# Products of weights with weights, written to idle PSUM banks, in TensorE's waits

## The reference

```
x = x + xattn(ctx_1024, layernorm(x), mask, ...)        # 2048 + 128 keys, 16 heads of 64
x = x + attn(layernorm(x), qw, kw, vw, ow)              # 16 heads of 32, causal, rotary
x = x + ffn(layernorm(x), ...)                          # see below
# ffn: mlp = silu(h @ Wg + bg) * (h @ Wu + bu) @ Wd + bd          (inner width 2048)
#      q = h @ Wq ; sim = q . keys ; top 8 of 64 on two sides, top 8 of their 64 sums
#      experts = sum over the 4 x 8 chosen of silu(h . down[i]) * softmax(score) * up[i]
#      returns mlp + experts
```

## Time and profile before

| | |
|---|---|
| median of 3 runs | 902.45 us (900.21 to 902.87) |
| the profiled execution: its own time | 903.4 us |
| the profiled execution: span | 901.6 us |
| mean granted TensorE clock over the span | 0.977 |
| TensorE busy | 855.2 us, 95% of the span, 6297 matmuls |
| VectorE, ScalarE, GpSimd busy | 64%, 49%, 39% |

### The profile page before, as it was taken

How to read it: one execution, slowest core, us unless ns; L and a number is a source line. 1 busy time by engine, 2 the same in 40 slices (tenths; PEclk the granted TensorE clock), 3 DMA queues, 4 the chain that set the end, 5 groups by cost and what they waited for, 6 DMA issues and landing times.

```text
span 901.6 us, 17320 instructions
## 1 busy us (share of the span) xinstructions
PE 855.2 (95%) x6297; PEld 800.6 (89%) x6297; DVE 581.5 (64%) x1540; ACT 437.5 (49%) x1017; POOL 349.0 (39%) x362
## 2 busy tenths in 40 slices
PE   3999999999999999999999999999998789998997
PEld 2899999999999999999999999999878689996885
DVE  7455557566577877665565666777766347755885
ACT  4575554554556564545446464445416024334652
POOL 5723634534464656446454523333002010003442
PEclk9999999999999999999999999999996779999999
DMA  5446336465466677675655656877577255932310
GB/s 189 167 155 199 134 107 233 177 241 218 177 233 239 218 256 259 215 254 189 245 183 211 233 189 229 329 272 259 192 282 336 77 214 218 375 135 95 113 48 24
DMA packets 71110, 183.04 MB, mean 203 GB/s; under 512 B 6337, under 2 KB 19569, under 8 KB 65009
## 3 DMA queue, kind: packets, MB, share of 16 engines
q1 hardware_dynamic: 70928, 181.90, 56.5%
q10 hardware_dynamic: 96, 0.02, 0.0%
HBM read 130.00 MB, written 50.86 MB: 201 GB/s over the span
## 4 chain that ended last, share of the span: by engine, by line
PE 81%; DVE 8%; issue 4%; ACT 3%; DMA 2%; POOL 1%; SPq 0%; DVEq 0%; ACTq 0%; POOLq 0%
PE pJ L1621 14%; PE pJ L1623 14%; PE pJ L1622 14%; PE pV L1751 7%; PE pS L1729 4%; PE pT L1737 3%; PE pS L1737 3%; PE pT L1729 2%; PE pS L1621 2%; PE pS L1623 2%; PE pS L1622 2%; PE pX L1652 1%; DVE late L1578 1%; PE pV L1621 1%; DMA WS<-w_split 1%
## 5 line engine op out<-in xcount | busy, mean ns | idle before, releaser
L1621 PE MATMUL pJ<-WV,XT 128*128 128x256 f32 x544 | 158.6, 292 | 0.1
L1622 PE MATMUL pJ<-WV,XT 128*128 128x256 f32 x544 | 153.8, 283 | 0.0
L1623 PE MATMUL pJ<-WV,XT 128*128 128x256 f32 x544 | 153.7, 283 | 0.0
L848 ACT ACTIVATE SP<-SP,xneg 128x768 f32<-128x768 f32 (+1 forms) x96 | 85.8, 895 | 120.1 <-DVE xneg L1200 120.1
L1621 PE MATMUL pJ<-XT,WK 128*128 128x384 f32 (+1 forms) x384 | 126.9, 331 | 3.8 <-DVE VT L1096 2.8
L1623 PE MATMUL pJ<-XT,WK 128*128 128x384 f32 (+1 forms) x384 | 125.2, 326 | 0.0
L1622 PE MATMUL pJ<-XT,WK 128*128 128x384 f32 (+1 forms) x384 | 125.1, 326 | 0.0
L1096 DVE TENSOR_TENSOR KT<-pJ,KT 128x384 fp32r<-128x384 f32 x96 | 51.0, 534 | 88.9 <-ACT KT L825 88.5
L1621 PEld LDWEIGHTS pJ<-WV,XT 128*128 128x128 f32 x544 | 104.1, 191 | 0.8 <-DVE KT L1096 0.3
L1622 PEld LDWEIGHTS pJ<-WV,XT 128*128 128x128 f32 x544 | 104.2, 192 | 0.0
L1623 PEld LDWEIGHTS pJ<-WV,XT 128*128 128x128 f32 x544 | 104.0, 191 | 0.0
(11 more groups left out here) (364 smaller groups left out, 2189.3 us busy)
## 6 DMA issues: line engine op xcount, KB each, us to landing
WS<-w_split SPq DMA_DIRECT2D x14, 2048.0 KB, 8.7
WV<-wv_split SPq DMA_DIRECT2D x20, 1024.0 KB, 7.5
WK<-wk_split SPq DMA_DIRECT2D x40, 512.0 KB, 4.4
w_split<-wkst SPq DMA_DIRECT2D x40, 512.0 KB, 3.3
w_split<-wvst SPq DMA_DIRECT2D x40, 512.0 KB, 4.0
XA<-w_split SPq DMA_DIRECT2D x4, 2048.0 KB, 12.7
xraw<-in_ctx SPq DMA_DIRECT2D x7, 768.0 KB, 5.5
wk_split<-WK SPq DMA_DIRECT2D x8, 512.0 KB, 4.0
```

The costliest lines, as they stand in the source:

```text
L848: ac.activation(SP[:, I % 2, h, 0:w], SP[:, I % 2, h, 0:w], ACT.Exp, bias=xneg[:, I % 2, h:h + 1], scale=XSC, accum_out=total).then_inc(c_ ...
L1621: te.matmul(dst, a(HI), b(HI), start=start, stop=False)
L1622: te.matmul(dst, a(HI), b(LO), start=False, stop=False)
L1623: return te.matmul(dst, a(LO), b(HI), start=False, stop=stop)
```

## The change

A helper `occupy(bank, weights, moving, n)` issues n matmuls whose operands are weights that lie in SBUF already, and whose result, in a bank that nobody reads at that time, is overwritten by the next real work. There are 56 of them, each 512 columns wide, in TensorE's program: 10 before the first query, 20 in the self-attention, 16 before and 5 after the last turn of normalised rows, and 5 before the key search. The semaphore waits that they need are added, and the wait for block 6 moves up with them. No other engine's program changes.

```diff
+            def occupy(bank, weights, moving, n):
+
+                for _ in range(n):
+                    te.matmul(bank, weights, moving, start=True, stop=True)
+
+            first_q = WQs[:, 0, HI, :, :].rearrange("p k n -> p (k n)")
             x_turn(0, 0)
             x_turn(0, 1)
+            pe.wait_ge(c_wqh, 1)
+            occupy(pS[:, 0, :], WQs[:, 0, HI, 0, :], first_q, 4)
             latent(0)
             latent(1)
+            occupy(pS[:, 0, :], WQs[:, 0, HI, 0, :], first_q, 2)
             latent(2)
             x_turn(0, 2)
             latent(3)
             x_turn(0, 3)
+            occupy(pS[:, 0, :], WQs[:, 0, HI, 0, :], first_q, 4)
             queries(0)
...
             turn_weights(0)
+            weight_ready(5)
+            pe.wait_ge(s_vh, 2)
+            occupy(pJ[:, 0, :], slot4(5, HI)[:, 0, 0:P], slot4(5, HI)[:, 0, :], 4)
             turn_weights(1)
+            pe.wait_ge(s_tl, 5)
+            occupy(pX[:, :], slot4(5, HI)[:, 0, 0:P], slot4(5, HI)[:, 0, :], 4)
             scores(1)
             weigh_values(0)
             weigh_values(1)
+            occupy(pJ[:, 1, :], slot4(5, HI)[:, 0, 0:P], slot4(5, HI)[:, 0, :], 4)
             turn_weights(2)
             turn_weights(3)
             weigh_values(2)
             weigh_values(3)
+            pe.wait_ge(s_p2h, 3)
+            occupy(pJ[:, 1, :], slot4(5, HI)[:, 0, 0:P], slot4(5, HI)[:, 0, :], 4)
             turn_weights(4)
             turn_rows(AO, 0, s_ao, 1)
             turn_weights(5)
             weigh_values(4)
             weigh_values(5)
+            occupy(pJ[:, 1, :], slot4(5, HI)[:, 0, 0:P], slot4(5, HI)[:, 0, :], 4)
             turn_weights(6)
...
             turn_rows(hn, 0, s_src, 3)
+            weight_ready(6)
+            occupy(pS[:, 0, :], slot4(6, HI)[:, 0, 0:P], slot4(6, HI)[:, 0, :], 16)
             turn_rows(hn, 1, s_src, 4)
+            occupy(pS[:, 0, :], slot4(6, HI)[:, 0, 0:P], slot4(6, HI)[:, 0, :], 5)
             pe.wait_ge(s_tl, 10)
-            weight_ready(6)
...
             pe.wait_ge(s_kl, 1)
+            occupy(pT[:, 1, :], HT[:, HI, 0, 0:P], HT[:, HI, 0:2, :].rearrange("p k t -> p (k t)"), 5)
             pe.wait_ge(s_q2l, 2)
```

## The result

| | before | after |
|---|---|---|
| median | 901.36 us (896.33 to 907.27, 10 runs) | 894.94 us (892.81 to 895.94, 10 runs) |
| ratio of the two | | 0.9923, 95% interval 0.9900 to 0.9946 |
| the profiled execution: own time, span | 903.4, 901.6 us | 892.87, 891.1 us |
| granted TensorE clock over the span | 0.977 | 0.995 |
| TensorE matmuls | 6297 | 6353 |

A forecast was written before the change was run, and what follows sets the result against it. TensorE, busy 95% of the span, was taken as the bound, with 40.8 us at half clock. Gains of 9.1 + 2.05 + 1.25 = 12.4 us took the profiled 903.4 to 891.0; median forecast 890.5, range 888 to 901.

The forecast's parts named there:

- the chance of 0.56: The forecast itself: the fillers hold the clock at every place, 890.5 us, own range 888.5 to 892.5.
- Rivals 1, 2 and 4: 1 and 2 have their own lines; 4: the fillers hold the clock nowhere, 908.8 us, chance 0.04.
- rival 3: Clock holds but falls at the new 2.25 us wait before `add_tile(0)`, losing 1.7 to 3.4: 893 us, chance 0.13.
- the mixing's end 19 us after the scores' start: Sign of being right in the self-attention, whose term was a gain of 9.1 us.
- The term that had no row: Self-attention: `weigh_values` at full clock takes half its time, 6.95 us gained; possible gain nothing to 6.95.
- The waits for DVE: Self-attention: TensorE waits 0.3 at `weigh_values(2)`, 0.45 at the turn of AO, 0.3 at `weigh_values(6)`, 1.05 us in all.
- 2.05 + 1.25 = 3.3: Gains in us from full clock: 2.05 at the last norm and query, 1.25 at the key search.
- moves as a whole: After the key search: DVE's `top_sides(0)`, 736.17 to 742.17, shifts earlier without a gap.
- I count 0 to 0.1 ... delay nothing by over 0.1.: Start: first query 1.1 us shorter but 0 to 0.1 gained; the ten fillers lie in TensorE's waits.
- Nothing later was at the low clock: After the key search and first of the MLP: no further low-clock stretch, and weight transfers move along.
- Rival 1: Clock falls near 682 anyway, stays low until the mixing; later places work: 905.5 us, chance 0.13.
- Rival 2: Clock holds at first, falls halfway through the self-attention, say before `turn_weights(4)`: 898 us, chance 0.14.

The follow-up runs named there:

- e3: Kernel before with only the twenty self-attention fillers added: 895.95 us, ratio 0.9942.
- e4: Kernel before with only the 26 fillers around the last turn and before the key search added: 899.44 us, ratio 0.9975.
- e1: Changed kernel without its ten fillers of the start: 891.98 us, ratio 0.9900 to the kernel before.
- e11: The changed kernel once more, only a comment added, on the same chip as e12: 894.98 us, ratio 0.9918 to the kernel before.
- e12: e1 once more, only a comment added, on the same chip as e11: 892.59 us, ratio 0.9893 to the kernel before.
- e2: Kernel before with only the ten fillers of the start added: 903.0 us, ratio 1.0006.
- e10: Changed kernel with only the last four of its ten start fillers, in front of the first query: 891.14 us, ratio 0.9879 to the kernel before.
- e8: Changed kernel without start fillers, each self-attention group replaced by eight transposes of a weight tile: 892.57 us, ratio 0.9911 to the kernel before.
- e7: Changed kernel without start fillers and without the two self-attention groups around turn_weights(1): 895.8 us, ratio 0.9939 to the kernel before.
- e5: Changed kernel without start fillers and without the three self-attention groups in the chain: 896.14 us, ratio 0.9938 to the kernel before.
- e6: Changed kernel without start fillers, two instead of four fillers in each of the three self-attention groups in the chain: 889.72 us, ratio 0.9883.

## Why the prediction was right, and where it was not

**The mechanism held.** The granted clock was 1.00 from 678 to 744 in the profile of the changed kernel; e3 and e4 show that the fillers of each part hold it at their own place. This was the case with the chance of 0.56. Rivals 1, 2 and 4 did not come about in it; rival 3, a fall at the widened wait before `add_tile(0)`, did not either, and that wait came to no more than 0.5 us, since `top_sides(0)` ended sooner than I had counted.

**How near the number came is in part luck.** On the profiled executions 891.0 was forecast and 892.87 measured, but the single errors are larger than this 1.9: the start lost 2.95 and the self-attention gave 1.2 less than its term, against 1.77 and 1.34 that came in without a term. The median, 894.94, is held by the wide range, 888 to 901, which was made to take in rivals that did not come about.

**The self-attention.** "the mixing's end 19 us after the scores' start": 19.2, and 19.2, 19.2 and 19.2 in e1, e11 and e12. (The prediction's sum has 18.3 for the same stretch, and its 701.1 is 0.1 later than 682.7 plus 18.3.) The term that had no row, `weigh_values` at the full clock, was taken as half, 1.8 a stretch, and is 1.86 to 1.97. A group of fillers stands at 1.01, not 0.92. The waits for DVE came out as 0.3, 0.3 and, with four a group, too small to be listed at the turn of AO; but the 4.3 us of DVE there are the chain, and TensorE's second group is hidden under them. I had paid for three groups and should have paid for two. In sum the stretch is 0.9 us longer than the 18.3 forecast from the late start of the scores. The start of the scores moved by 0.7 and not 0.4, since the first group took 1.18 us, not 0.92.

**Norm, query and search.** 2.05 + 1.25 = 3.3 forecast, 3.23 measured, and the last turn still waits for DVE's O (0.9 us in the waits of TensorE), not for a filler. Beside it there was a gain with no term: `top_sides(0)` "moves as a whole", I wrote, and it shrank from 6.00 to 4.23 us. In the kernel before, these are its last steps on DVE, and what ran on POOL at the time (from the groups of the stretch 736 to 743, mean ns of one behind the busy time):

```profile
L754 POOL TENSOR_TENSOR O<-xres,O 128x512 f32<-128x512 f32 x2 | 2.6, 1311 | 19.5 <-DMA O<-in_L_ffn_bd 19.5
```

```profile
739.73 0.87 DVE tail L1483
...
740.70 1.45 DVE late L1485
```

In the changed kernel they take 0.20 and 0.34. POOL's two additions start 3.1 us after the search's copy in the kernel before and fall on L1483 and L1485; in the changed kernel they start 5.2 us after it (731.8), behind them. In e2 and e3, which lack the fillers of norm and search, they start 3.2 and 3.0 us after it and L1483 takes 1.00 and 0.73; in all eleven profiles with these fillers they start at least 4.1 us after, and it takes 0.20. So DVE's steps take longer when they coincide with POOL's additions (which take 2.58 us there and 2.53 apart from them), and the change parts them: DVE comes earlier to its steps, while POOL's additions wait for a transfer (O from in_L_ffn_bd) and do not come earlier by as much. The gain is worth 1.8 us where it arises, and it reaches the end: from L1552 to DVE's first step at L1578, near the experts, all fourteen profiles take the same 76.6 to 76.8 us.

**The step that failed is the start.** "I count 0 to 0.1 ... delay nothing by over 0.1." Taking the ten fillers out gains 3.0 us (e1 against 894.94) and 2.4 on one chip (e12 against e11). What was wrong in it is the assumption that fillers in waits cost only what they delay. The first query did get its 1.1 us (its products at 0.12, where they took 0.21 in the kernel before, although the granted clock reads 1.00 there), and nothing of it was kept, as forecast. What I had not asked is what the clock does next when the query is done early. Behind the query and the first keys, TensorE waits for ACT's normalised latents: 0.60 us in the kernel before, 2.24 in the first profile of the changed one. After this wait the clock was down for the first values, whose products took 0.21 instead of 0.12, in both profiles of the changed kernel and in e2 (waits of 2.24, 1.90 and 1.98 us). I had looked for falls behind every wait in the middle of the kernel, and not in the part where I had counted the fillers as free.

The other half of that profile's 2.95 us is that nmr ended at 25.12 instead of 23.63. DVE's instructions ahead of it, in the kernel before and then in the changed one:

```profile
20.58 0.76 DVE L1096 TENSOR_TENSOR XT<-Oacc,XT 128x256 fp32r<-128x256 f32 x2
21.26 1.22 DVE L1096 TENSOR_TENSOR WV<-wvst,WV 128x1024 fp32r<-128x1024 f32 x1
```

```profile
20.99 1.84 DVE L1096 TENSOR_TENSOR XT<-Oacc,XT 128x256 fp32r<-128x256 f32 x2
22.75 2.30 DVE L1096 TENSOR_TENSOR WV<-wvst,WV 128x1024 fp32r<-128x1024 f32 x1
24.97 0.15 DVE L1296 SCALAR_TENSOR_TENSOR nmr<-mv,rstd 128x3 f32<-128x3 f32 x1
```

The low part of WV took 2.30 us and not 1.22, but it is not what made nmr late: nmr itself took 0.15 instead of 1.23, so the two together take as long as before. DVE was 1.49 us late when it began with WV, and 1.1 of that came in the step ahead, 1.84 instead of 0.76. POOL is busy for 3.9 of the 4 us beside it in both kernels; its step at L637 took 1.30 us where it took 1.88 before. So which of the two engines is held up seems to hang on how their steps fall on each other. It did not recur in e2 or e11 (keys at 46.88 and 46.61 instead of 48.16); in these the turns of the latents stood at 0.69 us, as before, and only in the first profile at 0.44. What recurred is the fall of the clock, some 1.5 us.

Two things stay open. In e10 TensorE had as little to do in that wait (1.70 us; 0.30 us busy in 24 to 26, as against 0.18 in e11), its query was at 0.12 a product from about 20.8 on, and the clock did not fall; why it falls behind ten fillers and not behind four, one profile of each doesn't tell, only their medians speak. And of the 2.4 to 3.0 us in medians this one fall explains about 1.5. Where else the clock was down, the profiles do not show, but the runs' granted clocks do say that it was: their mean is 0.9945 in e11 and 0.9967 in e12, 0.9952 in the changed kernel's first ten runs and 0.9972 in e1, and 0.002 of 892 us is 1.8 us (an estimate).

**The base.** The sum was made on an execution of 903.4 us, and the forecast for the changed kernel's own was 891.0; its profiled one took 892.87. The medians lie differently: over the 27 runs of the first set the kernel before went from 895.39 us at a granted clock of 0.986 to 905.88 at 0.975. 0.011 of 902 us is 9.9 us of full-speed time, about the whole of the difference of 10.5. The profiled execution has all three falls in full and a mean of 0.977. So, about, have most: 19 of the 27 runs are at 0.975 to 0.980. The other eight are at 0.982 to 0.986 and took 895.4 to 899.4 us. In those some of the time at the low clock must be absent, though no profile shows which, and there the fillers have less to win. Of the changed kernel the profiled execution is the second fastest of ten. So the two profiles differ by 10.5 us and the medians by 6.4, where 12.4 were forecast. Without the start's fillers it is 9.6 (e1) and 10.4 (e12). The Trainium skill (TensorE: Matmul & The Clock Gate, Part 1) says that how many matmuls run at the low clock at the start of a kernel varies from run to run. The runs here agree in that the mean granted clock of one kernel varies, 0.975 to 0.986; but the three falls that this kernel's profile shows, 40.8 us in all, lie far behind the start.

**Nothing later was at the low clock** held for the kernel before only. In the profiles of the changed kernel and of all others but e3 and e8 a fall stands near the start of the experts (from 810.0 us in the changed kernel), where the kernel before had 1.00. From DVE's first step at L1578 to the end it is 82.8 us in the three profiles without that fall and 83.4 to 84.0 in the eleven with it: 83.40 in the changed kernel, 82.76 before, which is 0.64 of the 0.83 us that are lost to the end. TensorE's wait for DVE (L1578) ahead of this place is 1.74 us in all fourteen, so the wait alone does not decide whether the clock falls. What does, no run tells.

**The rivals' prices.** Rival 1 assumed that after a fall near 682 the clock stays low until the mixing, and came to 905.5. e7 is its place and its fall, without the two first groups, and ran at 895.8: the groups in the chain raise the clock again. Its side of the forecast, slower than before, was therefore priced too high, and its chance of 0.13 for slower with it. Rival 2 was well priced in kind, 898: e5, 896.14, is the fall halfway, without the three groups in the chain and without the start's fillers.

**A better version.** e6 is best, 889.72 us, ratio 0.9883, but with one run of six 10 us slower. e10, four a group and only the last four fillers at the start, has 891.14 at 0.9879 and no such run in six. The intervals overlap, so neither is shown to be the better; either would be taken before the change as made. The two edits together were not tried.

## What to carry to other kernels

Where TensorE bounds a kernel and a stretch of narrow matmuls stands at half clock behind a wait, a few matmuls of no use in that wait, and a few among the narrow ones, can win more than they cost: here 27.9 us became 19.2 with 20 of them, in five groups of which one lay hidden under DVE's work. Look in every place, the harmless ones too, at what TensorE does after the fillers: where the work behind them ends sooner and the wait after it grows (here from 0.60 to about 2 us), the clock can fall behind that wait, and the work that it slows was fast before (here 2.4 to 3.0 us lost in medians, the fall itself some 1.5 of it, for 1.1 that nobody waited for). And take the spread of the kernel before as part of the base: a profile in which every fall happened overstates what holding the clock gives in the median.

## What the runs showed of the hardware

- In the self-attention, groups of eight float32 transposes of 128 x 128 (0.87 to 1.06 us, e8) held the granted clock at 1.00 as well as groups of four float32r matmuls of 512 columns (0.92 to 1.18 us): 19.0 against 19.2 us.
- A group of four wide matmuls at 1.2 GHz, among narrow ones, was followed by a rise: in e7 after 7 us at 0.50, where the same narrow work without the group stayed there for 27 us (e4). Each is one profile.
- The spread between executions of the kernel before is mostly the clock's: 895.39 us at 0.986, 905.88 at 0.975; with the fillers 892.81 to 895.94 at 0.993 to 0.998.
- The same wait of TensorE, 1.74 us for DVE (L1578), was followed by a fall of the clock in eleven profiles and by none in three; such a fall made the rest of the kernel 0.6 to 1.2 us longer.
- DVE took longer beside POOL's work at some steps: its conversion of 128 x 64 integers 0.87 instead of 0.20 us, its addition of 128 x 256 1.45 instead of 0.34 in the chain. At the start, with both busy in both kernels, it was now the one and now the other: DVE's low part of 128 x 1024 took 2.30 and POOL's step at L637 1.30 us in the changed kernel's first profile, 1.22 and 1.88 in the kernel before.
